# First head group projected straight onto its stack rows at the start of a decoder layer kernel

## What is computed

```
def _L0_attn_ref(x, Wq, Wk, Wv, Wo):
    def proj(W):
        return (x @ W).reshape(B, N, H, 2 * hd).transpose(0, 2, 1, 3)
    q = proj(Wq)
    k = proj(Wk)
    v = proj(Wv)
...
    scores = (jnp.einsum('bhnd,bhmd->bhnm', q_r, k_r) + jnp.einsum('bhnd,bhmd->bhnm', q_i, k_i)) / jnp.sqrt(jnp.float32(hd))
    causal = jnp.tril(jnp.ones((N, N), dtype=bool))
    scores = jnp.where(causal[None, None], scores, -jnp.inf)
    probs = jax.nn.softmax(scores, axis=-1)
...
x = x + _L0_attn_ref(_layernorm(x, axis=-1), L0_attn_Wq, L0_attn_Wk, L0_attn_Wv, L0_attn_Wo)
```

## Time and profile before

| | |
|---|---|
| median of 3 runs | 820.2 us (820.03 to 820.55) |
| profiled execution: its span, first to last instruction | 819.2 us |
| mean granted TensorE clock in the span | 0.991 |
| busy share PE / DVE / POOL / ACT | 94% / 77% / 58% / 49% |
| chain that ended last | PE 59%, DMA 18%, DVE 13% |
| moved by DMA | 70.56 MB |

### The profile page before, as it was taken

How to read it: one execution, slowest core, us unless ns; L and a number is a source line. 1 busy time by engine, 2 the same in 40 slices (tenths; PEclk the granted TensorE clock), 3 DMA queues, 4 the chain that set the end, 5 groups by cost and what they waited for, 6 DMA issues and landing times.

```text
span 819.2 us, 16261 instructions
## 1 busy us (share of the span) xinstructions
PE 769.2 (94%) x5757; PEld 528.7 (65%) x5757; DVE 631.8 (77%) x1251; ACT 402.6 (49%) x760; POOL 472.8 (58%) x428
## 2 busy tenths in 40 slices
PE   8788999999999999999999999999999997998998
PEld 7555565765566566666666666665766674477996
DVE  3544555457769897899879997999788989699874
ACT  5123555555555466646746573646464556542111
POOL 5000000031966789677868686878876796976442
PEclk9997999999999999999999999999999999999999
DMA  5886666866685668566756675667567670100001
GB/s 186 111 104 89 94 78 84 136 84 85 86 136 78 91 85 135 71 91 105 92 100 89 103 92 100 88 103 95 85 86 110 85 110 8 60 14 7 33 14 39
DMA packets 47982, 70.56 MB, mean 86 GB/s; under 512 B 4898, under 2 KB 22579, under 8 KB 47923
## 3 DMA queue, kind: packets, MB, share of 16 engines
q1 hardware_dynamic: 46898, 69.52, 56.7%
q10 hardware_dynamic: 1024, 0.26, 0.2%
HBM read 14.98 MB, written 4.19 MB: 23 GB/s over the span
## 4 chain that ended last, share of the span: by engine, by line
PE 59%; DMA 18%; DVE 13%; issue 4%; ACT 3%; POOL 1%; SPq 1%; ACTq 0%; DVEq 0%; POOLq 0%
PE misc L524 21%; DMA stack_k<-k_lo 17%; PE exp_bank L524 15%; PE acc_bank L524 10%; PE max_bank L524 9%; PE sum_bank L524 3%; DVE neg_max L1225 2%; DVE score_rows L1237 2%; DVE seg_max L1225 1%; DVE ln_raw L1203 1%; SPq L455 1%; DVE head_out L1237 1%; ACT max_row L903 1%; PE misc L574 1%; DVE k_lo L1231 1%
## 5 line engine op out<-in xcount | busy, mean ns | idle before, releaser
L950 ACT ACTIVATE probs<-exp_bank 128x512 f32<-128x512 f32 x320 | 188.4, 592 | 199.6 <-PE exp_bank L524 196.8
L1225 DVE TENSOR_REDUCE neg_max<-max_bank 128x1 f32<-128x512 f32 (+1 forms) x192 | 130.2, 683 | 88.9 <-PE max_bank L524 88.0
L1600 POOL TENSOR_TENSOR prod<-head_probs,ctx_sb 128x256 f32<-128x256 f32 (+1 forms) x100 | 185.0, 1883 | 2.2 <-POOL head_probs L1595 0.5
L524 PE MATMUL max_bank<-stack_k,stack_q 96*128 96x384 f32 (+3 forms) x512 | 155.2, 364 | 16.7 <-DMA stack_k<-k_lo 9.4
L524 PE MATMUL acc_bank<-probs,values 128*32 128x512 f32 (+3 forms) x1024 | 158.5, 447 | 4.1 <-ACT log_sum L961 2.1
L314 POOL TENSOR_TENSOR prod<-x1n,ctx_sb 128x256 f32<-128x256 f32 (+1 forms) x104 | 158.8, 1558 | 4.3 <-ACT x1n L910 4.3
L524 PE MATMUL sum_bank<-probs,ones 128*32 128x512 f32 (+3 forms) x1024 | 157.8, 444 | 0.0
L524 PE MATMUL exp_bank<-stack_q,stack_k 97*128 97x384 f32 (+3 forms) x512 | 149.3, 354 | 2.0 <-DVE wf_lo L1195 1.3
L524 PEld LDWEIGHTS exp_bank<-stack_q,stack_k 97*128 97x128 f32 x512 | 83.9, 194 | 56.4 <-issue 27.4
L1540 POOL TENSOR_TENSOR ln_var<-ln_mv,eps 128x4 f32<-128x4 f32 x21 | 4.4, 212 | 196.1 <-DVE ln_mv L1211 196.1
L1225 DVE TENSOR_REDUCE seg_max<-max_bank 128x4 f32<-128x512 f32 x128 | 86.8, 683 | 29.6 <-PE max_bank L524 27.8
(11 more groups left out here) (185 smaller groups left out, 1413.4 us busy)
## 6 DMA issues: line engine op xcount, KB each, us to landing
stack_q<-q_hi SPq DMA_DIRECT2D x64, 256.0 KB, 5.1
stack_k<-k_hi SPq DMA_DIRECT2D x64, 256.0 KB, 9.5
stack_q<-q_lo SPq DMA_DIRECT2D x32, 256.0 KB, 7.0
stack_k<-k_lo SPq DMA_DIRECT2D x32, 256.0 KB, 10.8
x_in<-in_x SPq DMA_DIRECT2D x9, 512.0 KB, 5.5
ctx_sb<-in_ctx SPq DMA_DIRECT2D x32, 128.0 KB, 3.1
x<-in_x SPq DMA_DIRECT2D x7, 512.0 KB, 10.1
out<-y_sb SPq DMA_DIRECT2D x5, 512.0 KB, 3.3
```

Source lines behind the costliest of these rows:

```text
L524: return nc.tensor.matmul(*args, **kw)
L950: nc.scalar.activation(probs[:, (UNITS * g + n) % PTR, :], exp_bank[n % 2][:, :], ACT.Exp, scale=SCALE).then_inc(exp_done, 1)
L1225: vec.tensor_reduce(o, v, axis=AX_X, op=ALU.max, negate=True).then_inc(max_taken, 1)
L1600: last = gp.tensor_tensor(pv_prod[:, COFF[j]:COFF[j + 1]].rearrange("p (q d k) -> p q d k", q=4, k=keys), head_probs[:, 4 * j:4 * j + 4, N ...
```

## The change

Group 0 no longer goes over `q_hi`, `q_lo`, `k_hi`, `k_lo` and the six DMAs. Its weights are copied so that each head's 32 columns stand three times side by side (`first_heads`, `repeat_weights`); with these 96 columns a projection gives the result three times over, on partitions 0 to 95, where the stack wants it. ACT copies all 96 rows as high part into the stack (`direct_high_part`), DVE then overwrites the 32 rows that are to hold the low part (`direct_low_part`). That is done for each head and for q and k apart: 8 projections of 6 matmuls in three PSUM banks that nothing else uses yet. The repeated weights lie in stack slot 3 and in `x2t_hi`, `x2t_lo`, which are free until later.

Group 1 is projected in pass (-1, 1), ahead of the direct projections, and group 2 in pass (-1, 2); pass (-1, 3) projects nothing. The weights are split in another order: group 1, the repeated ones of group 0, values, groups 2 and 3, and last the ordinary ones of group 0. Most fillers of the filling are gone.

```diff
         def stages(i, g):
...
-            return {"C": group(0), "B": group(2), "A": group(3), "M": group(1), "N": group(-1)}
+            staged = {FIRST_SPLIT: (0, 1), FIRST_PASS: (0, 2), SECOND_PASS: None}.get((i, g), group(3))
+            return {"C": group(0), "B": group(2), "A": staged, "M": group(1), "N": group(-1)}
...
-        FIRST_PASS = (-1, 2)
-        IDLE_FIRST, IDLE_TURN, IDLE_SPLIT, IDLE_STACK = 66, 10, 26, 22
-        IDLE_LOW, IDLE_MAXIMA, IDLE_ROW = 12, 1, 9
+        FIRST_SPLIT, FIRST_PASS, SECOND_PASS = (-1, 1), (-1, 2), (-1, 3)
+        FIRST_VALUES, FIRST_STAGED = (2, 4), (6, 7)
+        IDLE_FIRST, IDLE_TURN = 66, 10
+        IDLE_MAXIMA, IDLE_ROW = 1, 9
...
+        def first_heads(c, which):
+            return w_raw[:, c, which * W:which * W + P].rearrange("p (h o d) -> p h o d", h=G, o=1) \
+                .to_broadcast([P, G, 3, D])
+        direct_bank = (*exp_bank, sum_bank)
+        DIRECT = [(h, which) for h in range(G) for which in (0, 1)]
...
+            def project_direct(n):
+                h, which = DIRECT[n]
+                bank = direct_bank[n % 3]
+                wait(pe, direct_lo, n - 2)
+                k = 0
+                for c in range(CC):
+                    for wpart, xpart in split_terms(direct_w_hi, direct_w_lo, xt_hi, xt_lo):
+                        last = mm(bank[0:STACK, :], wpart(c)[:, which, h, :], xpart[:, c, :],
+                                  start=(k == 0), stop=(k == 5))
+                        k += 1
+                last.then_inc(direct_psum, 1)
...
-                    if (i, g) == FIRST_PASS:
-                        keep_busy(acc_bank, IDLE_SPLIT)
-                        pe.wait_ge(w_lo_ready, 2)
-                        for half in (0, 1):
-                            project_v(values_pair(i, g)[1], half)
-                        pe.wait_ge(w_lo_ready, 3)
-                        for which in (0, 1):
-                            project_qk(st["A"][1], which)
-                        keep_busy(acc_bank, IDLE_STACK)
...
+                            if (i, g) == FIRST_PASS and unit < G:
+                                pe.wait_ge(direct_lo, 2 * (unit + 1))
+                            elif unit == 0:
                                 pe.wait_ge(stacked, n_stack.up(16 * STACK_DMAS))
...
-                            keep_busy(acc_bank, IDLE_LOW if n == 2 else IDLE_MAXIMA)
+                            keep_busy(acc_bank, IDLE_MAXIMA)
+                        if (i, g) == FIRST_PASS and n in FIRST_VALUES:
+                            pe.wait_ge(w_lo_ready, 3)
+                            project_v(values_pair(i, g)[1], FIRST_VALUES.index(n))
+                        if (i, g) == FIRST_PASS and n in FIRST_STAGED:
+                            pe.wait_ge(w_lo_ready, 4)
+                            project_qk(st["A"][1], FIRST_STAGED.index(n))
...
+                            if n == 2 and (i, g) == FIRST_SPLIT:
+                                pe.wait_ge(w_lo_ready, 2)
+                                for direct in range(len(DIRECT)):
+                                    project_direct(direct)
...
+            def direct_high_part(n):
+                h, which = DIRECT[n]
+                act.wait_ge(direct_psum, n + 1)
+                copy(direct_stack(which)[0:STACK, 0, h, :], direct_bank[n % 3][0:STACK, :]).then_inc(direct_hi, 1)
...
+                    if (i, g) == FIRST_SPLIT:
+                        for direct in range(len(DIRECT)):
+                            direct_high_part(direct)
                         other_weights()
+                        split_rows(0)
...
+            def direct_low_part(n):
+                h, which = DIRECT[n]
+                rows = slice((1 + which) * D, (2 + which) * D)
+                part = direct_stack(which)[rows, 0, h, :]
+                dve.wait_ge(direct_hi, n + 1)
+                vec.tensor_tensor(part, direct_bank[n % 3][rows, :], f32(part), ALU.subtract).then_inc(direct_lo, 1)
...
-                        if st["A"] and n in (2, 3) and not stack_early(i, g):
+                        if (i, g) == FIRST_PASS and n in (8, 9):
+                            low_part(n - 8)
+                        elif st["A"] and n in (2, 3) and not stack_early(i, g) and (i, g) != FIRST_PASS:
...
+                    if (i, g) == FIRST_SPLIT:
+                        value_weights()
+                        for direct in range(len(DIRECT)):
+                            direct_low_part(direct)
                         other_weights()
+                        dve.wait_ge(w_hi_ready, 5)
+                        split_rows(0)
```

More of the change, by code:

```diff
@@ L912, in layernorm, with split_rows, repeat_weights @@
                 last.then_inc(ln_done[which], 1)
+            def split_rows(g):
+                for c in range(CC):
+                    last = copy(rows_of(by_row(w_hi, c), g), rows_of(by_head(w_raw, c), g))
+                last.then_inc(w_hi_ready, 1)
+            def repeat_weights():
+                for c in range(CC):
+                    for which in (0, 1):
+                        last = copy(repeated(direct_w_hi(c)[:, which, :, :]), first_heads(c, which))
+                last.then_inc(w_hi_ready, 1)
+            def direct_high_part(n):
+                h, which = DIRECT[n]
+                act.wait_ge(direct_psum, n + 1)
+                copy(direct_stack(which)[0:STACK, 0, h, :], direct_bank[n % 3][0:STACK, :]).then_inc(direct_hi, 1)
             nc.scalar.preload_act_table_set("natural_log_exp_and_others")
@@ L918, in _ @@
             act.wait_ge(w_loaded, 48)
-            for c in range(CC):
-                last = copy(first_rows(by_row(w_hi, c)), first_rows(by_head(w_raw, c)))
-            last.then_inc(w_hi_ready, 1)
+            split_rows(1)
             def keep_values(pair, half):
@@ L1472, in _ @@
             dve.wait_ge(w_hi_ready, 1)
-            for c in range(CC):
-                last = vec.tensor_tensor(first_rows(by_row(w_lo, c)), first_rows(by_head(w_raw, c)),
-                                         f32(first_rows(by_row(w_hi, c))), ALU.subtract)
-            last.then_inc(w_lo_ready, 1)
+            split_rows(1)
             turn.batches(dve, body, N_BATCH)
```

56 lines of the change are left out of this document (43 added, 13 removed).

## The result

The changed kernel is **slower**: 830.1 us (826.1 to 834.4, four runs) beside 820.1 us, a ratio of 1.0112 [1.0084 to 1.014]. Measured again it took 826.7 us (ten runs) beside 822.1 us (28 runs) on the same chip, 1.0048 [1.0025 to 1.007]; both intervals lie above the 0.2% that can be told from no change. The forecast was 816.2 us, and even the upper end of its range, 822.3, is too low. The profiled execution of the changed kernel took 826.1 us, with a span of 824.3. It is the fastest of the four; the two slowest, 832.8 and 834.4, were not profiled, and their mean granted clock is 0.979 and 0.980 beside 0.985, so they ran longer at half clock. What follows is about the 5.1 us between the two profiled spans, not the whole of the 10.

The account below looks back on a forecast made before the run. The prediction took the filling's chain of stack-DMA rounds, PE's waits and a half-clock stretch as the bound, with PE busy afterwards. U0 +0.1 and clock -4.1 gave -4.0 from 820.2: 816.2 us, range 814.8 to 818.

Parts of the forecast that it names:

- Start of the direct projections: In the filling: 48 direct matmuls start at 17.2 without a wait, 0.228 us each, 10.9 us, ending at 28.1.
- the slower rival: Direct projections run at half clock after idle PE from 17.2 to 19.0: 6.9 us more, 823.1 us; chance 0.17.
- Added wait on DVE: Pass (-1, 2): PE's unit three waits for DVE's first reduction until 35.2, 4.4 us idle; the clock falls.
- `max_ready` at 49.1: End of group 0's maxima in pass (-1, 2): ready at 46.7, or 49.1 with the half-clock cost.
- The 2.4 us taken for half clock: Pass (-1, 2): assumed cost of a half-clock stretch behind PE's wait for DVE, from a span of 1.7 to 5.1.
- has no projection and no DMA wait left: Pass (-1, 3): takes 6.2 us after the maxima, so pass (0, 0) begins at 55.3 instead of 54.09.
- the wait at U0: Pass (0, 0): group 2's transfers land near 58, so 1.10 us of DMA wait goes; U0 ready at 61.85.
- The clock stays at 1.00 in pass (0, 0): Dense projection replaces the idle time ahead of U0, so the half-clock stretch from 64.4 to 74.6 goes: minus 4.1 us.
- the forecast's own rival: The clock falls in pass (0, 0) all the same, behind 1.79 us of idle PE: 820.3 us, no change; chance 0.22.
- Behind 2.61 us of idle PE the clock did not fall: Before the first score unit, in the trace before: 2.61 us idle did not suffice at 31.75; counted against the half-clock direct projections.
- the row from 65.18 to 74.60: Pass (0, 0) before the change: cited as agreeing that the throttled clock is the default and activity releases it.
- What the filling gains is handed on to the end almost one to one: After the filling, from about 80 us: PE is busy nine tenths or more, so gains or losses reach the end.

Follow-up runs that it names:

- row_first: Changed kernel with group 2's k-row transfers issued only after group 0's max row has landed; 821.1 us, ratio 0.9968 to the kernel before.
- group2_late: Changed kernel with group 2 projected and stacked in pass (-1, 3) again, as before the change; 822.8 us, ratio 1.0007 to the kernel before.
- both: Changed kernel with the edits of row_first and weights_late together; 816.9 us, ratio 0.9938 to the kernel before.
- both_filled: The kernel of both with 38 more fillers in four idle times of PE in the filling; 812.95 us, ratio 0.9893 to the kernel before.
- before_third: The kernel before, unedited, run again for a third trace; 824.6 us (one run).
- before_code: Kernel before with its 66 first fillers of 256 columns written as 33 of 512; 823.0 us, ratio 1.0013 to the kernel before.
- before_filled: Kernel before with fillers ahead of group 2's first and third score units in pass (0, 0) and two sets at the end; 815.8 us, ratio 0.994.
- weights_late: Changed kernel with DVE's splitting of weights for groups 2, 3 and 0 moved later; 820.6 us, ratio 0.9978 to the kernel before.

## Why the prediction was wrong, step by step

- *Start of the direct projections at 17.2, 10.9 us for the 48, end at 28.1*: right. First at 17.19, 0.230 between them, the last ends at 28.4; neither ACT nor DVE made PE wait, so the slower rival (half clock in the direct projections) did not occur.
- *Added wait on DVE, 35.2, with a fall of the clock*: right, 4.58 us of idle PE ended at 35.27, half clock from 34.4.
- *`max_ready` at 49.1*: right, `turn_maxima` starts at 48.47. The 2.4 us taken for half clock were good: with the clock kept it starts at 46.05.
- *Pass (-1, 3) "has no projection and no DMA wait left", so pass (0, 0) begins at 55.3*: **this is the step that failed.** PE had done the last maxima at 54.8, but pass (0, 0) also needs the max row, and that is a DMA. I moved group 2's six transfers up to about 43 to 58, counted them for the wait at U0, and did not ask what else is sent in that time. The row lands at 57.8 and PE stands for 3.1 us. Taking the transfers out of its way took 5.6 us off the median, and 3.9 when group 2 went back to its old place. The trace of before had the sign: its row, issued at 42.9 behind group 1's transfers, took 5.1 us to land, the next one behind group 2's 4.2, and those after it 1.8; it cost nothing there, as PE needed it only at 54.09. Kernel before, 42 to 47 us:

```profile
stack_q<-max_row ACTq DMA_DIRECT2D x1, 8.0 KB, 5.1
```

- *The clock stays at 1.00 in pass (0, 0), -4.1*: wrong, and not by the late row alone. Behind the row's wait the clock fell at 58.3 for 3.4 us. Without that wait it fell all the same, behind the 1.78 us before U2: at 65.4 for 3.4 us in row_first, at 66.4 for 6.8 in group2_late, at 60.3 for 3.4 in both. That is the forecast's own rival, which it gave 0.22; with fillers at that place (both_filled) the clock stayed at 1.00. U0 itself had no wait for its stack, as forecast, but came 4 us late. The 4.1 was also a single execution's: in two of the five traces with the old filling as it was (before_third, before_code) the stretch is 3.4 us long instead of 10.2.
- *Behind 2.61 us of idle PE the clock did not fall*: true of the one trace that the forecast had. In four of the five other traces of the old way (before_filled with them) it falls there, between 31.4 and 33.2. And the row from 65.18 to 74.60, which the prediction takes as agreeing that activity releases the clock, shows PE busy for 9.42 of 9.42 us at 0.50: it shows a low clock behind a wait, and no release while PE was busy.
- *What the filling gains is handed on to the end almost one to one*: wrong by 2 us between 180 and 349 us, 0.7 of it by loads of PE's code inside the stack's transfers, 0.8 where DVE's add meets POOL's product, and 0.6 just ahead of that, for which no run shows a cause; and wrong behind 690 us, where 3.4 us go with half-clock stretches that lie elsewhere in each execution, of before too. The forecast had no term for either.

So the sum -4.0 became -0.3 in the filling, and 5.4 us were lost later: +5.1 between the two spans. With the late row and the late weights mended, and fillers on both sides, the direct projection is worth 3.4 us, give or take 2. That this is near the 4.0 of the forecast is luck: the forecast had its gain from the clock in pass (0, 0), and fillers give that to the old way as well; what is left goes with first exponentials 5 us earlier (48.95 beside 54.06), less what is lost at 122 to 130.

## What to carry to other kernels

When a group of transfers is moved up, list every other transfer that is issued in the time it now fills, the small ones above all: here an 8 KB row issued behind 1.5 MB landed as late as the 1.5 MB, though it has a queue of its own. When work that an engine did in idle time is put ahead of a reduction that PE waits for, move it behind the reduction; a filler saved the clock here but not the wait. And before a gain of half a per cent is believed, compare several traces of the same kernel: where stretches of half clock come and go, one trace is a sample.

## What the runs showed of the hardware

- A transfer of 32 packets on one queue stood for 6.5 us while 461 packets of another went by; with nothing on that queue (group2_late) its first packet moved 1.3 us after the issue.
- The length of PE's program changes the time of passes some 180 us later: 33 matmuls fewer at the start moved a 16 KB load of code into the stack's transfers, +0.4 us in one pass and +0.2 in the next, at the same places in seven of the eight traces with the shorter program (in the eighth, weights_late, half clock lies over the first).
- An add of DVE (128x256) that starts just ahead of a product of POOL takes 0.4 to 0.7 us, and one that starts just behind it 2.1 to 2.5 (17 traces).
- In the end part the granted clock is 0.50 for 3.4 to 10.2 us at places that change between executions of one program; in two traces of before PE was busy for 67.6 of 70 us by the profile, once at a mean clock of 1.00 and once at 0.90.
